# First layer's gate/up of a two-layer FFN kernel: seven of its eleven tiles as seven block products each

## The chip, the cores and the metric

One core of a Trainium2 chip runs the whole program. The metric is the device time of one execution in microseconds (us); three executions of the kernel before give 455.81, 456.37 and 456.49, median 456.37.

## The reference, cut to what matters

Two layers are applied to x of 8 x 128 tokens (1,024) by 512 features, each as x + ffn(cond(x)). The part that changes is the first gated FFN, whose weights come as 4-bit numbers ("nibbles"), packed by eight in a 32-bit word, with a zero point and a scale for each group of 128 input rows.

```python
def _dequant(qw, qz, sc, g_idx):
    wq = qw[:, None, :] >> shifts[None, :, None] & NIB
    zq = qz[:, :, None] >> shifts[None, None, :] & NIB   # + 1.0
    return sc[g_idx] * (wq - zq[g_idx])
w_gu = _dequant(qweight_gu, qzeros_gu, scales_gu, g_idx_gu)   # 512 x 2752
inter = einsum('bsh,hf->bsf', y, w_gu)                        # y = _L0_cond_ref(x, ...)
gate, up = inter[..., :1376], inter[..., 1376:]
h = silu(gate) * up
w_d = _dequant(qweight_down, qzeros_down, scales_down, g_idx_down)
x = x + einsum('bsf,fh->bsh', h, w_d)
x = x + _L1_ffn_ref(_L1_cond_ref(x, ...), ...)                # plain weights, 512 -> 1792 -> 512
```

## The kernel before

Everything is held transposed: features on the 128 partitions, 1,024 tokens along the row, in two halves of 512 (one PSUM bank each). fp32 accuracy comes from splitting every operand into a rounded part (hi, made by ScalarE, helper `hi`, L658) and a remainder (lo, made by VectorE, helper `lo`, L967) and taking three products: w_hi v_hi, w_hi v_lo, w_lo v_hi (`mm3`, L1443, L1444, L1447). A 128x128 block of weights against 1,024 tokens is thus six matmuls of 512 columns.

The order on each engine is the order in which the code issues it; engines are tied by semaphores alone. The stages on TensorE: ten warming matmuls; routing, LoRA and base product of the first condition layer, which leaves y in the banks 0/1, 4/5, 6/7 and 2/3 (`lora`, in this order; each increments `s_y`); the first gate/up, eleven tiles of 128 hidden features (FT0 = 11); the first down projection in six chunks (`d0_tile`, chunks of 4, 4 and 3 tiles for each of two pairs of outputs); the second condition layer (`z_product`); the second gate/up in 14 tiles, which is already done by seven block products each (`product`, `p_1` to `p_7`); the second down projection, in block products too.

A first gate/up tile (`gate_up`) is eight weight blocks (gate and up, four of each), 48 matmuls. It uses banks 0 to 3 for even tiles and 4 to 7 for odd ones. Around it:

- SyncE loads the packed weights of one tile at a time (`load_qw`, L416), and in the last third of the stage the packed down weights (`load_qd`, L434, through three slots, the fourth load waiting for `s_dn`, the count of dequantized down rows), then x again for the residual (L440).
- GpSimd gathers, by indirect DMA (helper `gather`, L579), four times 256 scales a tile (`scales_gu`) and two rows of down tables after it (`tables_dn`).
- VectorE takes the nibbles out of the bytes (L1080), adds the zeros (L1084) and multiplies by the scales (`dequant_gu`, L1087, increments `s_wf`); makes lo of the weights (`w_lo`), multiplies silu(gate) by up (`gu_step`, L1115), makes lo of the result, and dequantizes the eleven rows of down weights (`dequant_dn`, L1095 to L1109) between the last tiles. `w_lo_dn(e)` makes lo of the weights of down chunk e.
- ScalarE makes hi of y, weights and result, and silu (L715).

The tiles 2 to 9 run in a hardware loop on SyncE, TensorE, ScalarE and VectorE.

The second gate/up shows what a block tile is. Weights are a 2 x 2 arrangement of 256 x 128 blocks A11, A12, A21, A22, activations one of B11, B12, B21, B22. GpSimd makes four sums of weight blocks (`sums`, L616 to L621: S1 = A21+A22, S3 = A11-A21, S2 = S1-A11, S4 = A12-S2), four sums of activation blocks are made once, and seven products of six matmuls each give what eight gave. Products share banks, so ScalarE copies partial results out between them (`snap_1`, `snap_5`, `snap_2`) and VectorE adds them (`c_11`, `c_12`, `c_22`), and the last product of a tile, `p_4`, is issued behind `p_1` of the next tile. Its hi and lo of weights are 1,792 columns wide, where a plain tile has 1,024.

## Time and profile before

| | us |
|---|---|
| median of three executions (455.81 to 456.49) | 456.37 |
| the profiled execution's own time | 457.44 |
| its span, first to last instruction | 455.6 |
| TensorE busy in the span | 449.1 |
| VectorE, ScalarE, GpSimd busy | 319.3, 195.2, 172.8 |
| first gate/up stage on TensorE, 45.01 to 165.62 | 120.6 |

The page's times are of one execution. Busy time counts overlapping matmuls once. 'Idle before' is the time that the engine stood still ahead of a group, and the arrow says what ended it. Columns of an instruction row: start, duration, engine, line, operation, output <- input, shape, count, and idle time before it in brackets. A matmul of 512 columns is shown as 0.39 us, but the next starts 0.23 us after it, since they are pipelined.

### The profile page before, as it was taken

How to read it: one execution, taken by the hardware profiler on the slowest of the kernel's cores; microseconds unless marked ns; L12 is line 12 of the kernel's file. 1: busy time of each engine (PE TensorE's matmuls, PEld its weight loads, DVE VectorE, ACT ScalarE, POOL GpSimd, SP SyncE). 2: the span in 40 equal slices, each digit the busy share in tenths (PEclk: the TensorE clock that was granted, in tenths of full speed). 3: DMA queues.
4: the chain of work that ended last, by engine and by line, in shares of the span. 5: the costliest groups of instructions: out<-in, count | busy, mean ns of one | idle time of the engine just before them, and what ended most of it. 6: DMA issues, size and time to landing. Idle time of an engine off the chain costs nothing.

```text
span 455.6 us, 5596 instructions
## 1 busy us (share of the span) xinstructions
PE 449.1 (99%) x1988; PEld 366.5 (80%) x1988; DVE 319.3 (70%) x420; ACT 195.2 (43%) x247; POOL 172.8 (38%) x160
## 2 busy tenths in 40 slices
PE   8999999999999999999999999999999999999996
PEld 4688887888888888888888778888888888888885
DVE  3864845555557998746687768868788578999921
ACT  4513423233222224235666756556465545474200
POOL 3254774743330000900002779795987500000000
PEclk9999999999999999999999999999999999999999
DMA  8262443441315236276358824947749146885623
GB/s 263 81 192 77 133 142 95 137 124 58 127 46 208 71 91 280 82 288 229 106 195 304 331 81 143 303 129 270 260 140 306 62 161 255 312 307 174 221 102 130
DMA packets 32357, 79.93 MB, mean 175 GB/s; under 512 B 3232, under 2 KB 17728, under 8 KB 30800
## 3 DMA queue, kind: packets, MB, share of 16 engines
q1 hardware_dynamic: 28128, 68.05, 43.2%
q0 software_dynamic: 3632, 10.84, 7.5%
q10 hardware_dynamic: 576, 0.79, 0.5%
q8 instruction: 10, 0.16, 0.1%
q14 instruction: 11, 0.09, 0.1%
HBM read 58.95 MB, written 20.72 MB: 175 GB/s over the span
## 4 chain that ended last, share of the span: by engine, by line
PE 96%; DMA 2%; ACT 1%; SPq 0%; issue 0%; DVE 0%
PE ps L1443 15%; PE ps L1447 15%; PE ps L1444 15%; PE ps L1612 10%; PE ps L1613 10%; PE ps L1614 10%; PE ps L1715 5%; PE ps L1714 5%; PE ps L1716 5%; DMA res<-in_xT 2%; PE ps L1595 2%; PE ps L1593 2%; PE ps L1594 2%; PE ps L1601 1%; ACT act_hi L658 0%; SPq L398 0%
## 5 line engine op out<-in xcount | busy, mean ns | idle before, releaser
L1443 PE MATMUL ps<-h_hi,ring_hi 128*128 128x512 f32 x264 | 102.7, 389 | 0.0
L1444 PE MATMUL ps<-h_lo,ring_hi 128*128 128x512 f32 x264 | 102.7, 389 | 0.0
L1447 PE MATMUL ps<-h_hi,ring_lo 128*128 128x512 f32 x264 | 82.3, 389 | 0.8 <-issue 0.8
L579 POOL DMA_INDIRECT raw<-in_sc_gu,idx_gu x44 | 47.9, 1088 | 42.1 <-DVE ring_lo L967 20.6
L1443 PEld LDWEIGHTS ps<-h_hi,ring_hi 128*128 128x128 f32 x264 | 49.6, 188 | 10.8 <-issue 0.5
L1447 PEld LDWEIGHTS ps<-h_hi,ring_lo 128*128 128x128 f32 x264 | 49.6, 188 | 10.7 <-issue 0.5
L1444 PEld LDWEIGHTS ps<-h_lo,ring_hi 128*128 128x128 f32 x264 | 49.6, 188 | 10.3
L1612 PE MATMUL ps<-zt_hi,ring_hi 128*128 128x512 f32 x140 | 54.6, 390 | 0.1
L658 ACT ACTIVATE ring_hi<-raw 128x1792 fp32r<-128x1792 f32 (+1 forms) x23 | 32.1, 1398 | 52.3 <-PE ps L1447 30.9
L1614 PE MATMUL ps<-zt_hi,ring_lo 128*128 128x512 f32 x140 | 54.5, 389 | 0.0
L1613 PE MATMUL ps<-zt_lo,ring_hi 128*128 128x512 f32 x140 | 54.5, 389 | 0.0
L967 DVE TENSOR_TENSOR ring_lo<-raw,ring_hi 128x1792 fp32r<-128x1792 f32 (+1 forms) x23 | 42.2, 1835 | 7.1 <-ACT ring_hi L658 7.1
L1115 DVE TENSOR_TENSOR sil<-sil,ps 128x1024 f32<-128x1024 f32 x11 | 13.4, 1221 | 35.9 <-PE ps L1447 25.7
L1612 PEld LDWEIGHTS ps<-zt_hi,ring_hi 128*128 128x128 f32 x140 | 26.3, 188 | 6.0 <-issue 0.5
L1614 PEld LDWEIGHTS ps<-zt_hi,ring_lo 128*128 128x128 f32 x140 | 26.3, 188 | 5.5
L1613 PEld LDWEIGHTS ps<-zt_lo,ring_hi 128*128 128x128 f32 x140 | 26.3, 188 | 5.4
L1714 PE MATMUL ps<-slot,wd 128*128 128x512 f32 x70 | 27.2, 389 | 0.0
L1716 PE MATMUL ps<-slot,wd 128*128 128x512 f32 x70 | 27.2, 389 | 0.0
L715 ACT ACTIVATE sil<-ps 128x1024 f32<-128x1024 f32 x11 | 11.3, 1027 | 31.3 <-PE ps L1447 21.0
L967 DVE TENSOR_TENSOR ad_lo<-ad_raw,ad_hi 128x1024 fp32r<-128x1024 f32 x15 | 19.4, 1328 | 5.5 <-ACT ad_hi L658 5.5
L1612 PE MATMUL ps<-ze_hi,ring_hi 128*128 128x512 f32 x56 | 22.1, 394 | 0.0
L1614 PE MATMUL ps<-ze_hi,ring_lo 128*128 128x512 f32 x56 | 21.8, 390 | 0.0
(218 smaller groups left out, 873.8 us busy)
## 6 DMA issues: line engine op xcount, KB each, us to landing
ad_raw<-in_w1T SPq DMA_DIRECT2D x8, 1024.0 KB, 4.9
wd<-down_weights SPq DMA_DIRECT2D x7, 1024.0 KB, 5.7
...
```

The lines of the kernel that those rows point to most:

```text
L579: pool.indirect_dma_start(dst, None, table, bass.IndirectOffsetOnAxis(ap=index, axis=0)).then_inc(done, 16)
L658: act.activation(dst, src, ACT.Copy).then_inc(done, 1)
L967: dve.tensor_tensor(dst, src, hi_part.bitcast(F32), ALU.subtract).then_inc(done_sem, 1)
L1443: pe.matmul(ps[:, bank + hf, :], w_hi, v_hi[:, t], start=first, stop=False)
L1444: pe.matmul(ps[:, bank + hf, :], w_hi, v_lo[:, t], start=False, stop=False)
L1447: ins = pe.matmul(ps[:, bank + hf, :], w_lo, v_hi[:, t], start=False, stop=last)
L1612: pe.matmul(ps[:, bank, :], ring1_hi[s][:, w], z_hi[:, t], start=first and k == 0, stop=False, skip_group_check=True)
L1613: pe.matmul(ps[:, bank, :], ring1_hi[s][:, w], z_lo[:, t], start=False, stop=False, skip_group_check=True)
L1614: ins = pe.matmul(ps[:, bank, :], ring1_lo[s][:, w], z_hi[:, t], start=False, stop=k == 1, skip_group_check=True)
L1714: pe.matmul(ps[:, bank, :], w_hi, v_hi, start=k == 0 and i in (1, 2, 3, 5), stop=False, skip_group_check=True)
L1715: pe.matmul(ps[:, bank, :], w_hi, v_lo, start=False, stop=False, skip_group_check=True)
L1716: return pe.matmul(ps[:, bank, :], w_lo, v_hi, start=False, stop=k == DH - 1, skip_group_check=True)
```

## The change

Tiles 2 to 8 of the first gate/up (BLOCK_TILES) are computed by seven block products of six matmuls; tiles 0, 1, 9 and 10 stay plain, with gate and up as functions of their own. For it:

- y is copied out of PSUM (`y_copy`), its four block sums are made by VectorE and split (`y_sum_hi`, `y_sum_lo`). TensorE waits with the first gate for the first of these copies, since its banks are read by it.
- GpSimd makes the weight sums of each block tile (`sums` with `blocks0`) between the gathers of scales. Weight and partial-result buffers are laid out anew.
- All packed weights of the stage are loaded by two DMAs at the start, their nibbles taken out in two VectorE instructions and the zeros added in three, where each tile had one of either.
- Gathers of down tables and loads of packed down weights wait for the last seventh product (`s_p[7]` >= 7). The reload of x is issued behind the load of row 4.
- The loops of this stage are gone on all engines; semaphores shared with the second layer's tiles count on from NS = 7.
- ScalarE makes hi of down chunk 2 before adapter 0, not behind it.

The diff, cut to its core:

```diff
+PLAIN = (0, 1, FT0 - 2, FT0 - 1)
+SC_KB = tuple((64, 112)[i % 2] if i != FT0 - 2 else 196 for i in range(FT0))
+
+
 HI_FRAME = (2, 3, 5, 6, 8, 9, 11)
...
+            return h_hi[:, YT + m, t], h_lo[:, YT + m, t]
+
+        def w_col(block, k):
+
+            if block in S_COL:
+                return S_COL[block] + P * k
+            return {B_A11: 0, B_S4: P, B_A12: 4 * P, B_A22: 5 * P}[block] + 2 * P * k
+
+        def blocks0(s):
+
+            w = raw0[s][:, 0:8 * P].rearrange("p (k g n) -> p k g n", k=KD, g=2)
+            s1, s2, s3 = (raw0[s][:, S_COL[b]:S_COL[b] + 2 * P].rearrange("p (k n) -> p k n", k=2) for b in (B_S1, B_S2, B_S3))
+            return w[:, 0:2, 1, :], w[:, 0:2, 0, :], w[:, 2:4, 0, :], w[:, 2:4, 1, :], s1, s2, s3, w[:, 0:2, 1, :]
+
         def g_bank(s, x):
...
-                load_qw(i, i)
-            with loop(sp, 0, (FT0 - 3) // 2) as j:
-                for s in range(2):
-                    need(sp, s_nib, 2 * j + s + 1)
...
             for k in range(3):
                 load_qd(k)
-            need(sp, s_wf, FT0)
-            sp.dma_start(res[:, :, :], a["xT"]).then_inc(s_xr, 16)
-
-
             sp.wait_ge(s_aok, 1)
             rows = [sp.value_load(aid[0:1, 2 * NBATCH + b:2 * NBATCH + b + 1], min_val=0, max_val=NBATCH - 1)
...
@@ -450,6 +487,11 @@
             for k in range(3, FT0):
                 sp.wait_ge(s_dn, k - 2)
                 load_qd(k)
+                if k == 4:
+                    sp.wait_ge(s_wf, FT0)
+                    sp.wait_ge(s_hm0, NS)
+                    sp.wait_ge(s_hm1, NS)
+                    sp.dma_start(res[:, :, :], a["xT"]).then_inc(s_xr, 16)
             sp.wait_ge(s_ring, FT0)
             for b in range(2):
                 load_adapter(b)
...
+            def sums(n, a21, a11, a12, a22, s1, s2, s3, s4):
+
                 pool.tensor_tensor(s1, a21, a22, ALU.add).then_inc(s_sum[1], 1)
                 pool.tensor_tensor(s3, a11, a21, ALU.subtract).then_inc(s_sum[3], 1)
                 pool.wait_ge(s_sum[1], n)
                 pool.tensor_tensor(s2, s1, a11, ALU.subtract).then_inc(s_sum[2], 1)
+                pool.wait_ge(s_sum[3], n)
                 pool.wait_ge(s_sum[2], n)
                 pool.tensor_tensor(s4, a12, s2, ALU.subtract).then_inc(s_sum[4], 1)
+
+            def blocks1(w):
+
+                return (w[:, i, :] for i in range(8))
+
+            for i in range(4):
+                scales_gu(i)
+            for i in BLOCK_TILES:
+                pool.wait_ge(s_wf, i + 1)
+                sums(sum_at("q", i), *blocks0(i % 2))
+                if i + 2 < FT0:
+                    scales_gu(i + 2)
+            pool.wait_ge(s_p[7], NS)
+            tables_dn(0, 5)
+            pool.wait_ge(s_ring, BLOCK_TILES[-1] + 1)
+            tables_dn(5, FT0)
 
...
-                need(act, s_ring, q - 1)
-                hi(ring_hi[:, s, 0:width], raw[:, s, 0:width], s_whi)
-
-            def w_hi_gu(i, s):
-                w_hi(i, s, 1024, s_wf, i + 1)
+            def y_copy(m, b, value):
+                act.wait_ge(s_ylo, value)
+                act.activation(halves(y_raw[:, m, :]), ps[:, b:b + 2, :], ACT.Copy).then_inc(s_yr, 1)
+
+            def y_sum_hi(i):
+                act.wait_ge(s_yt, i)
+                hi(y_sum(yt_hi, i), y_low(yt_raw, i), s_yth)
+
+            def w_hi(i):
+
+                if i in BLOCK_TILES:
+                    act.wait_ge(s_sum[3], sum_at("q", i))
+                    act.wait_ge(s_sum[4], sum_at("q", i))
+                    n = 14 * P
+                else:
...
-                for s in range(2):
-                    i = 2 * j + s
-                    gu_step(i, s, 0, lambda: w_hi_gu(i + 2, s))
-            gu_step(FT0 - 3, 0, 0, lambda: w_hi_gu(FT0 - 1, 0))
-            gu_step(FT0 - 2, 1, 0, lambda: w_hi_dn(0))
-            gu_step(FT0 - 1, 0, 0, lambda: None)
+            y_copy(3, 2, KD)
+            y_copy(1, 4, KD)
+            y_copy(2, 6, KD)
+            y_sum_hi(1)
+            silu(0)
+            y_sum_hi(2)
+            w_hi(2)
+            y_sum_hi(3)
+            y_sum_hi(4)
+            h_split(0)
+            silu(1)
+            for i in BLOCK_TILES:
+                y_snap_1(i)
+                w_hi(i + 1)
+                y_snap_5(i)
+                h_split(i - 1)
+                y_snap_2(i)
+                y_silu_0(i)
+                y_silu_1(i)
+            w_hi(FT0 - 1)
+            h_split(FT0 - 3)
+            silu(FT0 - 2)
+            w_hi_dn(0)
+            h_split(FT0 - 2)
+            silu(FT0 - 1)
+            h_split(FT0 - 1)
             w_hi_dn(1)
 
 
...
 
             def pre_split(g):
 
-                act.wait_ge(s_sum[3], g + 1)
-                act.wait_ge(s_sum[4], g + 1)
+                act.wait_ge(s_sum[3], sum_at("w", g))
+                act.wait_ge(s_sum[4], sum_at("w", g))
...
+            NIB_PARTS = ((0, 5), (5, FT0))
+
+            def nibbles(part):
+
+                i0, i1 = NIB_PARTS[part]
+                m = m16[:, i0:i1, :, :].rearrange("p i g w -> p (i g w)")
+                dve.tensor_scalar(m, m, sh16, 0x0F0F, ALU.logical_shift_right, ALU.bitwise_and).then_inc(s_nib, 1)
+
+            dve.wait_ge(s_sh, 16)
+            dve.wait_ge(s_qw, 32)
+            nibbles(0)
             dve.wait_ge(s_gTp, 1)
             dve.wait_ge(s_hAc, 1)
             dve.tensor_tensor(halves(hg_full), ps[:, 2:4, :], halves(hA_full), ALU.mult).then_inc(s_hg, 1)
+            nibbles(1)
             dve.wait_ge(s_hghi, 1)
             lo(hg_lo, hg_full, hg_hi, s_hglo)
...
-                n2 = nib_gu[s].bitcast(U16).rearrange("p (g w) -> p g w", g=2 * KD)
-                dve.tensor_tensor(n2, n2, zg16[:, :, bass.ds(i * 64, 64)], ALU.add).then_inc(s_n, 1)
-                need(dve, s_n, i + 1)
-                need(dve, s_raw["gu0"][s], (i - s) * 32 + 64)
-                dve.scalar_tensor_tensor(out=raw[:, s, :], in0=nib_gu[s], scalar=16.0, in1=raw[:, s, :], op0=ALU.subtract,
-                                         op1=ALU.mult).then_inc(s_wf, 1)
+            zg16 = zg.bitcast(U16).rearrange("p (g i w) -> p i g w", g=2 * KD, i=FT0)
+            ZERO_PARTS = ((0, 2), (2, 5), (5, FT0))
+
+            def add_zeros(part):
+
+                i0, i1 = ZERO_PARTS[part]
+                dve.wait_ge(s_nib, 2 if i1 == FT0 else 1)
+                dve.tensor_tensor(m16[:, i0:i1], m16[:, i0:i1], zg16[:, i0:i1], ALU.add).then_inc(s_n, 1)
+
+            def dequant_gu(i):
+
+                s = i % 2
+                dve.wait_ge(s_n, sum(i >= i0 for i0, _ in ZERO_PARTS))
+                need(dve, s_wlo, i - 1)
...
+                dve.wait_ge(s_s5, frame(i) + 1)
+                dve.tensor_tensor(snap0[i % 2][:, 2, :], ps[:, y_bank(i % 2, 0), :], snap0[i % 2][:, 2, :], ALU.add).then_inc(s_c22, 1)
+
+            def y_mul_0(i):
+                dve.wait_ge(s_silu0, frame(i) + 1)
+                dve.wait_ge(s_ring, i + 1)
+                dve.tensor_tensor(h_raw[:, i, first], snap0[i % 2][:, 0, :], ps[:, y_bank(i % 2, 0), :], ALU.mult).then_inc(s_hm0, 1)
+
...
                 dve.wait_ge(s_whi, Q["d0"] + e + 1)
                 lo(d0_ring(ring_lo, e), d0_unit(e), d0_ring(ring_hi, e), s_wlo)
 
 
-            dequant_gu(0, 0)
...
+            w_lo(0)
+            dequant_gu(1)
+            add_zeros(2)
+            w_lo(1)
             y_split(0, 0)
-            w_lo(0, 0, 1024)
             y_split(1, 4)
+            dequant_gu(2)
             y_split(2, 6)
             y_split(3, 2)
-            dequant_gu(1, 1)
-            w_lo(1, 1, 1024)
-            dequant_gu(2, 0)
-            for i in range(2):
-                gu_step(i, i, 0, Q["gu0"], lambda: w_lo(i + 2, i, 1024))
-                dequant_gu(i + 3, 1 - i)
-            with loop(dve, 1, FT0 // 2 - 1) as j:
-                for s in range(2):
-                    i = 2 * j + s
-                    gu_step(i, s, 0, Q["gu0"], lambda: w_lo(i + 2, s, 1024))
-                    dequant_gu(i + 3, 1 - s)
-            dequant_dn(0)
-            gu_step(FT0 - 3, 0, 0, Q["gu0"], lambda: w_lo(FT0 - 1, 0, 1024))
-            for k in range(1, 4):
+            b11, b12 = y_raw[:, 0:2, first], y_raw[:, 0:2, second]
+            b21, b22 = y_raw[:, 2:4, first], y_raw[:, 2:4, second]
+            dve.wait_ge(s_yr, 3)
+            dve.tensor_tensor(y_low(yt_raw, 1), b12, b11, ALU.subtract).then_inc(s_yt, 1)
+            dve.wait_ge(s_yr, KD)
+            dve.wait_ge(s_yt, 1)
+            dve.tensor_tensor(y_low(yt_raw, 2), b22, y_low(yt_raw, 1), ALU.subtract).then_inc(s_yt, 1)
+            dve.tensor_tensor(y_low(yt_raw, 3), b22, b12, ALU.subtract).then_inc(s_yt, 1)
+            dve.wait_ge(s_yt, 2)
+            dve.tensor_tensor(y_low(yt_raw, 4), b21, y_low(yt_raw, 2), ALU.subtract).then_inc(s_yt, 1)
+            y_sum_lo(1)
+            y_sum_lo(2)
+            gate_times_up(0)
+            w_lo(2)
+            dequant_gu(3)
+            y_sum_lo(3)
+            y_sum_lo(4)
+            h_split(0)
+            for i in BLOCK_TILES:
+                dequant_gu(i + 2)
+                if i > 2:
+                    y_mul_0(i - 1)
+                else:
+                    gate_times_up(i - 1)
+                w_lo(i + 1)
+                y_c_11(i)
+                h_split(i - 1)
+                y_c_12(i)
+                y_c_22(i)
+                y_mul_1(i)
+            y_mul_0(FT0 - 3)
+            w_lo(FT0 - 1)
+            h_split(FT0 - 3)
+            for k in range(4):
                 dequant_dn(k)
-            gu_step(FT0 - 2, 1, 0, Q["gu0"], lambda: w_lo_dn(0))
-            for k in range(4, 7):
+            gate_times_up(FT0 - 2)
+            w_lo_dn(0)
+            h_split(FT0 - 2)
+            for k in range(4, 8):
                 dequant_dn(k)
-            gu_step(FT0 - 1, 0, 0, Q["gu0"], lambda: dequant_dn(7))
+            gate_times_up(FT0 - 1)
+            h_split(FT0 - 1)
             w_lo_dn(1)
 
...
+                    c = slice(2 * P * k, 2 * P * k + P)
+                    ins = mm3(4 * s, ring0_hi[s][:, c], ring0_lo[s][:, c], y_hi[:, k, :], y_lo[:, k, :], k == 0, k == KD - 1)
+                if KD - 1 in ks:
+                    ins.then_inc(s_gate, 1)
+
+            def up(i):
+
+                s = i % 2
+                for k in range(KD):
...
+
+                bank = y_bank(s, x)
+                for k in range(2):
+                    c = w_col(W_OF[i], k)
+                    w_hi, w_lo = ring0_hi[s][:, c:c + P], ring0_lo[s][:, c:c + P]
+                    v_hi, v_lo = y_block(right, k) if isinstance(right, str) else (y_sum(yt_hi, right)[:, k], y_low(yt_lo, right)[:, k])
+                    pe.matmul(ps[:, bank, :], w_hi, v_hi, start=first_in_bank and k == 0, stop=False, skip_group_check=True)
+                    pe.matmul(ps[:, bank, :], w_hi, v_lo, start=False, stop=False, skip_group_check=True)
+                    ins = pe.matmul(ps[:, bank, :], w_lo, v_hi, start=False, stop=k == 1, skip_group_check=True)
+                return ins
+
+            def sum_ready(i):
+                pe.wait_ge(s_yth, i)
+                pe.wait_ge(s_ytl, i)
+
+            def y_p_1(i):
+                weights_ready(i)
+                if i < 4:
+                    pe.wait_ge(s_hm, i - 1)
+                need(pe, s_hm0, frame(i) - 1)
+                y_product(1, i % 2, 0, True, "b11").then_inc(s_p[1], 1)
+
+            def y_p_4(i):
+                sum_ready(4)
+                pe.wait_ge(s_c22, frame(i) + 1)
...
+                pe.wait_ge(s_s5, frame(i) + 1)
+                y_product(3, i % 2, 2, False, "b22").then_inc(s_p[3], 1)
+
+            def y_p_7(i):
+                sum_ready(3)
+                pe.wait_ge(s_s2, frame(i) + 1)
+                y_product(7, i % 2, 0, False, 3).then_inc(s_p[7], 1)
+
+            def banks_free(n):
+                pe.wait_ge(s_hm0, n)
+                pe.wait_ge(s_c11, n)
+                pe.wait_ge(s_c12, n)
+
+            weights_ready(0)
+            pe.wait_ge(s_yr, 1)
+            gate(0, range(KD), s_ylo)
+            pe.wait_ge(s_yr, 2)
+            up(0)
+            weights_ready(1)
+            pe.wait_ge(s_yr, KD)
+            gate(1, range(KD))
+            up(1)
+            for i in BLOCK_TILES:
+                y_p_1(i)
+                if i > BLOCK_TILES[0]:
...
+                y_p_3(i)
+                y_p_7(i)
+            weights_ready(FT0 - 2)
+            banks_free(NS - 1)
+            gate(FT0 - 2, range(1))
+            y_p_4(FT0 - 3)
+            gate(FT0 - 2, range(1, KD))
+            up(FT0 - 2)
+            weights_ready(FT0 - 1)
+            banks_free(NS)
+            gate(FT0 - 1, range(KD))
+            up(FT0 - 1)
 
             def d0_tile(e, k, m, hfs):
```

## Rows read from the trace of the kernel before

**Rows 1.** The page: busy time by engine, and the chain that ended last.
```profile
PE 449.1 (99%) x1988; PEld 366.5 (80%) x1988; DVE 319.3 (70%) x420; ACT 195.2 (43%) x247; POOL 172.8 (38%) x160
...
PE 96%; DMA 2%; ACT 1%; SPq 0%; issue 0%; DVE 0%
```

**Rows 2.** Timeline of TensorE at the first tile: starts of two groups of six.
```profile
45.01 0.39 PE L1443 MATMUL ps<-h_hi,ring_hi 128*128 128x512 f32 x1
...
46.37 0.39 PE L1443 MATMUL ps<-h_hi,ring_hi 128*128 128x512 f32 x1
```

**Rows 3.** Timeline of TensorE in tile 2, the first one in the loop.
```profile
70.40 0.39 PE L1447 MATMUL ps<-h_hi,ring_lo 128*128 128x512 f32 x1
71.54 0.39 PE L1447 MATMUL ps<-h_hi,ring_lo 128*128 128x512 f32 x1 [0.76 <-issue]
```

**Rows 4.** Timeline of ScalarE in the second gate/up: snap_1 of two tiles, between them hi, snap_5, snap_2.
```profile
299.59 0.60 ACT L832 ACTIVATE snap<-ps 128x512 f32<-128x512 f32 x1 [1.36 <-PE ps L1614]
301.04 1.71 ACT L658 ACTIVATE ring_hi<-raw 128x1792 fp32r<-128x1792 f32 x1 [0.84 <-PE ps L1614]
302.65 0.57 ACT L842 ACTIVATE snap<-ps 128x512 f32<-128x512 f32 x1
305.03 0.60 ACT L837 ACTIVATE snap<-ps 128x512 f32<-128x512 f32 x1 [1.81 <-PE ps L1614]
...
309.11 0.60 ACT L832 ACTIVATE snap<-ps 128x512 f32<-128x512 f32 x1 [0.85 <-PE ps L1614]
```

**Rows 5.** Groups of GpSimd by line and shape: busy, mean ns | idle before.
```profile
L579 POOL DMA_INDIRECT raw<-in_sc_gu,idx_gu x44 | 47.9, 1088 | 42.1 <-DVE ring_lo L967 20.6 <-issue 13.1 <-PE ps L1447 5.3
L617 POOL TENSOR_TENSOR raw<-raw 128x256 f32<-128x256 f32 x12 | 19.6, 1632 | 0.0
L621 POOL TENSOR_TENSOR raw<-raw 128x256 f32<-128x256 f32 x12 | 18.9, 1573 | 0.9
L619 POOL TENSOR_TENSOR raw<-raw 128x256 f32<-128x256 f32 x12 | 11.1, 929 | 0.0
L616 POOL TENSOR_TENSOR raw<-raw 128x256 f32<-128x256 f32 x12 | 10.2, 848 | 13.4 <-DMA raw<-in_gu 13.1
```

**Rows 6.** Timeline of GpSimd: a sum alone, a sum beside VectorE, two gathers.
```profile
260.53 0.74 POOL L617 TENSOR_TENSOR raw<-raw 128x256 f32<-128x256 f32 x1
...
181.13 1.64 POOL L616 TENSOR_TENSOR pre_raw<-pre_raw 128x256 f32<-128x256 f32 x1 [50.30 <-DVE ring_lo L967]
...
30.39 0.95 POOL L579 DMA_INDIRECT raw<-in_sc_gu,idx_gu  x1 [0.30 <-issue]
31.65 1.63 POOL L579 DMA_INDIRECT raw<-in_sc_gu,idx_gu  x1 [0.30 <-issue]
33.58 0.95 POOL L579 DMA_INDIRECT raw<-in_sc_gu,idx_gu  x1 [0.30 <-issue]
```

**Rows 7.** Timeline of VectorE beside them, and the first multiplication by scales.
```profile
180.97 6.25 DVE L967 TENSOR_TENSOR ad_lo<-ad_raw,ad_hi 128x1024 fp32r<-128x1024 f32 x4
...
31.23 1.23 DVE L967 TENSOR_TENSOR h_lo<-sil,h_hi 128x1024 fp32r<-128x1024 f32 x1 [1.13 <-ACT h_hi L658]
...
36.88 1.23 DVE L1087 SCALAR_TENSOR_TENSOR raw<-res,raw 128x1024 f32<-128x1024 uint8 x1 [3.30 <-DMA raw<-in_sc_gu,idx_gu]
```

**Rows 8.** Groups of VectorE by line and shape: busy, mean ns | idle before.
```profile
L967 DVE TENSOR_TENSOR ring_lo<-raw,ring_hi 128x1792 fp32r<-128x1792 f32 x12 | 28.8, 2396 | 5.8 <-ACT ring_hi L658 5.8
L967 DVE TENSOR_TENSOR h_lo<-sil,h_hi 128x1024 f32 x6 | 7.4, 1226 | 1.3 <-ACT h_hi L658 1.1 <-issue 0.2
L1084 DVE TENSOR_TENSOR res<-res 128x512 uint16<-128x512 uint16 x11 | 4.7, 426 | 1.0
L1258 DVE TENSOR_TENSOR snap<-ps,snap 128x512 f32<-128x512 f32 x14 | 9.7, 691 | 8.5 <-PE ps L1614 8.4
```

**Rows 9.** Timeline of ScalarE: hi of the first quarter of y.
```profile
41.13 1.03 ACT L658 ACTIVATE h_hi<-ps 128x1024 fp32r<-128x1024 f32 x1 [9.94 <-PE ps L1447]
```

**Rows 10.** Timeline of VectorE: first instructions of two down rows, then w_lo_dn(1).
```profile
150.25 0.48 DVE L1095 TENSOR_SCALAR dn_work<-dn_work,shifts 128x512 uint32<-128x512 uint32 x1
...
152.68 0.48 DVE L1095 TENSOR_SCALAR dn_work<-dn_work,shifts 128x512 uint32<-128x512 uint32 x1
...
170.66 1.23 DVE L967 TENSOR_TENSOR ring_lo<-dn_work,ring_hi 128x1024 fp32r<-128x1024 f32 x1
```

More of the change, by code:

```diff
@@ L40 @@
 FT1 = F1 // P
-CH0 = (6, 5)
 NPAIR = NBATCH // 2
@@ L332, in z_bank, with y_bank, frame, plain @@
             return Z_BANK[b]
+        def y_bank(s, x):
+            return 4 * s + x
+        def frame(i):
+            return BLOCK_TILES.index(i)
+        def plain(i):
+            return PLAIN.index(i)
+        def y_sum(t, i):
+            return t[:, i - 1]
+        def y_low(t, i):
+            return t[:, i % 4]
+        def y_block(b, k):
+            m, t = {"b11": (k, first), "b21": (2 + k, first), "b22": (2 + k, second)}[b]
+            return h_hi[:, YT + m, t], h_lo[:, YT + m, t]
[7 more added lines that the diff above has]
+            return w[:, 0:2, 1, :], w[:, 0:2, 0, :], w[:, 2:4, 0, :], w[:, 2:4, 1, :], s1, s2, s3, w[:, 0:2, 1, :]
         def g_bank(s, x):
@@ L355, in d0_unit, with table_group @@
             return tab_dn[:, k0:k0 + D0_CHUNK[c], BLK * pr:BLK * pr + BLK]
+        def table_group(k):
+            return sum(k >= sum(D0_CHUNK[:c]) for c in range(1, len(D0_CHUNK)))
         def d0_ring(ring, e):
@@ new lines, in h_split, with y_snap_1 @@
+            def h_split(i):
+                if i in BLOCK_TILES:
+                    act.wait_ge(s_hm0, frame(i) + 1)
+                    act.wait_ge(s_hm1, frame(i) + 1)
+                    hi(h_hi[:, i, :], h_raw[:, i, :], s_hhi)
+                else:
+                    act.wait_ge(s_hm, plain(i) + 1)
+                    hi(h_hi[:, i, :], sil[i][:, :], s_hhi)
+            def y_snap_1(i):
+                act.wait_ge(s_p[1], frame(i) + 1)
+                need(act, s_hm0, frame(i) - 1)
+                act.activation(snap0[i % 2][:, 0, :], ps[:, y_bank(i % 2, 0), :], ACT.Copy).then_inc(s_s1, 1)
@@ L958, in _, with mark @@
             done = [0]
+            def mark(ins):
+                done[0] += 1
+                return ins.then_inc(s_v, 1)
             def own(ins):
```

323 lines of the change are left out of this document (172 added, 151 removed).

## The prediction, made before the change was run

> **What bounds the kernel now.** I read the page's busy times first, then its chain: TensorE is busy in 449.1 of 455.6 us and holds 96% of the chain that ended last [rows 1]. So time goes only if TensorE gets less work, or if it stands still. Next its timeline: six matmuls, one weight block against 1,024 tokens, start 1.36 us apart (45.01 to 46.37) [rows 2]. In the whole stage it stands still once, in tile 2: a matmul starts at 71.54 where 70.40 + 0.23 = 70.63 was due, released by "issue", not by data, with hardly more than 0.9 us lost [rows 3]. No other engine holds it there. Last, the second gate/up, which already runs in block products: its snap_1 come at 299.59 and 309.11, 9.52 us apart, which is 7 x 1.36 [rows 4]. That stage is the pattern for what the new tiles do on TensorE, ScalarE and VectorE.
>
> **Part 1, fewer products: -9.5 us.** A plain tile is 8 x 1.36 = 10.88 us, a block tile 9.52 [rows 2, 4]. Seven tiles save 7 x 1.36 = 9.52 us, 42 of 1,988 matmuls. That a block product is no slower than its six matmuls is what the 9.52 us of the second layer show.
>
> **Part 2, no loop in this stage: -0.9 us.** The pause of 71.54 - 70.63 = 0.9 us lies in the loop's first pass, and the straight code around it has none [rows 3]. It could stay (straight code is longer to fetch), so 0 to -0.9; I take it whole.
>
> **Part 3, start of the stage: +0.8 us (0 to 2).** TensorE comes free for tile 0 at 45.01 [rows 2]. It now also waits for y_copy(0) on ScalarE, which waits for lo of the first y quarter on VectorE, and VectorE has both dequantizations, both w_lo and the zero additions queued ahead of that. The last release among these is a gather. GpSimd no longer waits for the router and can start scales right behind its last small DMA, near 26.3. A gather is issued each 1.25 us (30.39 to 31.65), some take 0.6 more [rows 6]; with one such in each four, tile 0's are out at 31.9 and tile 1's at 37.1. Landing: the last gather of tile 0 ended at 33.58 + 0.95 = 34.53 and VectorE went on at 36.88, 2.35 later [rows 6, 7]. So tile 1's scales are there at 39.4. Behind them: multiplication 1.2, zeros of six tiles, w_lo(1) 1.2, lo of y 1.2, y_copy 1.03 and two handovers of 0.1. The zeros: 512 columns of 16 bits took 0.43 [rows 8], some 0.15 of it fixed (estimate), so 3,072 take 1.8. Sum 39.4 + 6.6 = 46.0 less the overlaps of 0.1 to 0.2 between VectorE instructions: 45.8. Hi of y starts at 41.13 now [rows 9] and isn't the last. The nibble instructions lie before and behind the LoRA product, hidden by the wait for scales even if they take twice what I give them (1 us each). The two loads of 0.7 MB stand behind x in SyncE's queue; their cover is that nothing needs them before 27, and without it they would push this chain by their landing. The other copies of y are read in time: the first `up` needs banks 2/3 only 5.4 us later. The work behind (block sums of y, four 1,024-wide instructions each for sum, hi and lo, some 14 us in all) has the 21.8 us of tiles 0 and 1 as cover.
>
> **Part 4, block tiles beside GpSimd: +1.9 us (0 to 5).** VectorE per tile, with the rows' means: multiplication by scales 1.23, w_lo 2.4, lo of h 1.23, three adds and two products of about 0.7 each: 8.3 of 9.52 us [rows 7, 8]. ScalarE: 1.71 + 3 x 0.6 + 1.06 + 2 x 0.62 = 5.8 [rows 4]. Both fit. GpSimd is the tight one: four sums and four gathers. The means of the second layer's sums are 0.85 + 1.63 + 0.93 + 1.57 = 5.0 us; a gather is 1.09 + 0.30 of issue, four 5.5 [rows 5]. That is 10.5 us, more than the tile's 9.52. The means hold collisions: a sum is 0.74 alone and 1.64 beside VectorE instructions that read two SBUF tensors, one of 1.23 of which then becomes 6.25 / 4 = 1.56; a gather is 0.95 or 1.63 [rows 6, 7]. The lower bound is 4 x 0.74 + 4 x 1.25 = 8.0. In this loop VectorE's two-SBUF instructions are about 5 of 9.5 us, but shorter ones (1.2) than the 2.5 us ones that the second layer's sums run into. Placing them one by one: w_lo and lo of h fall on the gathers (+0.5 us each, less 0.1), the multiplication on one or two sums (+0.9 to +1.5). That gives 9.8 to 10.1; I take P = 9.9.
>
> What P costs: sums(3) can start only when VectorE has dequantized tile 3, behind the y work, at 62.7, and in collision takes 4 x 1.65, so ends at 69.3 (clock of before, part 3's shift left out). Sums(8), five rounds later, ends at 69.3 + 5P. Behind it until p_4(7) may start: hi 1.8, w_lo 2.0, c_11, lo of h, c_12, c_22: 7.0 us. Undisturbed, p_4(7) starts at 45.01 + 21.76 + 8.16 + 5 x 9.52 + 1.36 = 123.9. Delay = 69.3 + 5P + 7.0 - 123.9 = 5P - 47.6: 1.9 at 9.9; nothing at 9.5; 4.9 at 10.5. It comes as some 0.4 us per tile, with VectorE's c_22 ahead of p_4.
>
> The Trainium skill, GPSIMD Engine Reference, section Key points, says that GpSimd shares its SBUF interfaces with VectorE and contends with instructions that have two SBUF inputs; it speaks against moving sums into this stage. The trace agrees (0.74 against 1.64), and shows the gathers' instructions longer too. By that rule alone the sum would be nearer to P = 10.5, -3.3 us in all; by the placement above it is -6.3.
>
> **Part 5, down tables behind the tiles: +1.4 us (0 to 3).** Let Z be the end of p_7(8). New waits: GpSimd and SyncE for s_p[7] >= 7, behind which stand all down gathers, and on SyncE x's reload and the adapters. Four rows of gathers take 5.2 us and land 2.35 later: Z + 7.7. VectorE is free at Z + 6.5. A row costs 152.68 - 150.25 = 2.43 us [rows 10], four 9.7: Z + 17.4. Then gate_times_up(9), w_lo_dn(0) and lo of tile 9 (3 x 1.2), four more rows to Z + 30.7, then the product of tile 10, ready at Z + 23.3 but last in VectorE's queue, its hi and lo, and w_lo_dn(1): Z + 35.4. TensorE from Z: gate and up of tiles 9 and 10 and p_4, 17 x 1.36 = 23.1; down chunk 0, 8 x 1.36 = 10.9: it wants chunk 1 at Z + 34.0. It waits 1.4 us. Before, w_lo_dn(1) was done at 171.9 [rows 10] and wanted at 165.6 + 10.9 = 176.5, 4.6 us ahead; all of that cover is used. Next, chunk 2: rows 8 to 10 (7.3), hi and lo end at Z + 44.6, wanted at 46.3. Chunk 3, behind two adapters on both engines: 52.4 against 54.5. Both just hidden, as ScalarE makes chunk 2 before the adapter. Everything further hangs on TensorE's own counts and shifts with it. Rows 5 and on come behind x's 2 MB on SyncE (7.6 us) but are wanted at Z + 23 at the earliest.
>
> **Sum.** -9.5 - 0.9 + 0.8 + 1.9 + 1.4 = -6.3 us. Against the profiled execution's own time, 457.44 (span 455.6 and 1.84 around it), 451.1; the median of the runs is 1.07 lower, 456.37, which gives **450.1 us**.
>
> **The rivals.**
> 1. *All cover holds*: GpSimd needs no more than 9.5 us a tile, VectorE gets to the down rows in time. For it: 8.0 us without collisions [rows 6]. Against it: the means of 10.5 [rows 5]. Time 456.4 - 10.4 + 0 to 1.5: 446.0 to 447.5, centre 447.
> 2. *GpSimd at its means*, P = 10.5: 3.0 us more than my forecast, 453.1. For it: rows 5 as they stand, measured beside a like VectorE load.
> 3. *GpSimd paces the whole stage, slower than before*: the place is sums and gathers against VectorE, the price 5P - 47.6, and it decides from P = (47.6 + 8.2 + 0.9) / 5 = 11.3. If sums keep 5.0 and every gather takes 1.5 + 0.3 [rows 5, 6], P = 12.2, a delay of 13.4 instead of 1.9: 461.6. Against it: a mean gather is 1.09 with VectorE half busy.
> 4. *The saving isn't there*: block products leave a gap at each change of bank, so a tile takes 10.88 still. The second layer's 9.52 [rows 4] speaks against it; it would give 450.1 + 9.5 = 459.6.
>
> **How the numbers follow.** Forecast 0.50 (448 to 452), rival 1 0.24, rival 2 0.19, rival 3 0.04, rival 4 0.01, and 0.02 for nearly nothing gained. Differences under 0.2% (0.9 us) can't be told from no change here. Faster 0.93, same 0.02, slower 0.05. Range 446.6 to 454.0: it takes in rival 1's centre and rival 2, with parts 3 and 5 at their upper ends in part.
>
> **What would show it.** Tile 0 of gate/up starting on TensorE near 45.8; snap_1 of block tiles 9.5 apart up to tile 4 and about 9.9 from there; TensorE's waits named VectorE adds in the block tiles, about 2 us in all; one wait of 1 to 2 us for ring_lo at down chunk 1, and none at chunks 2 and 3; 1,946 matmuls; no pause by "issue" near 71. Wrong would make it: GpSimd sums beyond 5 us a tile, a wait for scales on VectorE that holds products behind it, instruction fetch in the straight code, or loads of packed weights that slow x at the start.

## The result, and the profile after

The changed kernel takes **461.09 us** (median of 4 runs, 460.69 to 463.71) against 456.38 (455.81 to 456.49) before: ratio 1.0118, 95% interval 1.008 to 1.0156. It is 1.2% slower where 1.4% faster was forecast. The profiled execution took 461.01 us, its span is 459.2. Ratios and intervals leave out the two executions that took over 1.5% more than the fastest of their kernel, one of before (463.34 us) and one of experiment 8 (457.44 us).

The page after: busy time, granted clock by slices, the chain that ended last, the costliest GpSimd group (busy, mean ns | idle before).
```profile
PE 444.0 (97%) x1946; PEld 358.4 (78%) x1946; DVE 343.7 (75%) x439; ACT 218.9 (48%) x283; POOL 216.9 (47%) x187
...
PEclk9999999999999998999999999999999999999999
...
PE 71%; POOL 15%; issue 7%; DVE 4%; DMA 1%; ACT 1%; POOLq 0%; ACTq 0%; DVEq 0%
...
L620 POOL DMA_INDIRECT scale<-in_sc_gu,idx_gu x44 | 59.9, 1361 | 12.3 <-issue 11.7
```
TensorE has 42 matmuls less, and its busy time is 5.1 us less than in [rows 1], not 9.5. It held 96% of the chain; now 15% is GpSimd's and 7% "issue". The same 44 gathers take 59.9 us of GpSimd instead of 47.9 [rows 5]. And one slice of the clock is under full speed; before, none was.

What TensorE waited for, by releaser (us in total, times, longest):
```profile
PE ps L1611 <- issue: 3.5, 1, 3.5
PE ps L1611 <- DVE h_lo L1067: 3.1, 1, 3.1
PE ps L1725 <- ACT snap L795: 3.1, 4, 1.3
```
Its timeline places them: tile 0, the four waits of the third product (p_3, which adds to the bank that snap_5 reads first; the first wait is shown, in tile 4), and down chunk 1.
```profile
47.66 0.47 PE L1611 MATMUL ps<-h_hi,ring_hi 128*128 128x512 f32 x1 [3.15 <-DVE h_lo L1067]
...
95.48 0.50 PE L1725 MATMUL ps<-h_hi,ring_hi 128*128 128x512 f32 x1 [1.33 <-ACT snap L795]
...
178.67 0.51 PE L1611 MATMUL ps<-h_hi,ring_hi 128*128 128x512 f32 x1 [3.48 <-issue]
```
And the windows of TensorE around them (window: its length, busy us and matmuls, granted clock, DMA share, GB/s):
```profile
47.66:164.15 116.49, 113.13 (x486) 1.00 0.28 91
164.15:178.67 14.52, 11.05 (x49) 1.00 0.61 216
178.67:182.10 3.43, 3.43 (x9) 0.54 1.01 420
```
From this the account. **Start:** 47.66 against 45.01 [rows 2], +2.65. **Stage:** gate and up of 11 tiles are 4 x 10.88 + 7 x 9.52 = 110.16 us of matmuls and took 116.49 (chunk 0 starts at 164.15), +6.33. The four waits show only half of that, 3.1 us: each is counted from the end shown for the matmul before, 0.16 us behind the time at which the next was due, and pauses of 0.1 to 0.2 us follow in the same product and the next, some 0.5 us a tile. The first matmuls of p_3 start at 95.48, 106.23, 117.20 and 128.15, 10.75, 10.97 and 10.95 us apart. **Down chunk 1:** wanted at 164.15 + 10.88 = 175.03, started at 178.67, +3.64. **Clock:** behind that stand TensorE ran 3.43 us at 0.54 of full speed, the lower of its two levels (1.2 GHz) for nearly all of it: 3.43 x 0.46 = +1.6. The sum is +14.2, less the 9.5 and 0.9 won: +3.8; the span grew by 3.6.

### The profile page after: what moved, and what is told of

Read it like the earlier page. It is cut to its first block, busy times and chain, and to the rows that moved or that the text cites. A ratio compares the mean times of both kernels' runs of the same rounds, so it can differ in the third digit from the quotient of the medians.

```text
span 459.2 us, 5528 instructions
## 1 busy us (share of the span) xinstructions
PE 444.0 (97%) x1946; PEld 358.4 (78%) x1946; DVE 343.7 (75%) x439; ACT 218.9 (48%) x283; POOL 216.9 (47%) x187
## 4 chain that ended last, share of the span: by engine, by line
PE 71%; POOL 15%; issue 7%; DVE 4%; DMA 1%; ACT 1%; POOLq 0%; ACTq 0%; DVEq 0%
PE ps L1865 10%; PE ps L1867 10%; PE ps L1866 10%; POOL scale L620 8%; PE ps L1611 6%; PE ps L1612 6%; PE ps L1615 6%; PE ps L1968 5%; PE ps L1967 5%; PE ps L1969 5%; PE ps L1848 2%; PE ps L1846 2%; PE ps L1847 2%; POOL raw L648 2%; POOL raw L651 2%
## 5 line engine op out<-in xcount | busy, mean ns | idle before, releaser
L1611 PE MATMUL ps<-h_hi,ring_hi 128*128 128x512 f32 x152 | 60.0, 395 | 6.6 <-issue 3.5
L620 POOL DMA_INDIRECT scale<-in_sc_gu,idx_gu x44 | 59.9, 1361 | 12.3 <-issue 11.7
L1612 PE MATMUL ps<-h_lo,ring_hi 128*128 128x512 f32 x152 | 59.9, 394 | 0.0
L1067 DVE TENSOR_TENSOR ring_lo<-raw,ring_hi 128x1792 fp32r<-128x1792 f32 (+1 forms) x23 | 45.5, 1978 | 17.6 <-ACT ring_hi L704 17.4
L704 ACT ACTIVATE ring_hi<-raw 128x1792 fp32r<-128x1792 f32 (+1 forms) x23 | 36.6, 1592 | 41.1 <-POOL raw L651 15.8
L1615 PE MATMUL ps<-h_hi,ring_lo 128*128 128x512 f32 x152 | 48.2, 392 | 0.0
L1611 PEld LDWEIGHTS ps<-h_hi,ring_hi 128*128 128x128 f32 x152 | 28.9, 190 | 13.4 <-issue 7.4
L1612 PEld LDWEIGHTS ps<-h_lo,ring_hi 128*128 128x128 f32 x152 | 29.0, 191 | 6.0
L1615 PEld LDWEIGHTS ps<-h_hi,ring_lo 128*128 128x128 f32 x152 | 28.8, 190 | 6.1
L1865 PEld LDWEIGHTS ps<-zt_hi,ring_hi 128*128 128x128 f32 x140 | 26.3, 188 | 6.3 <-issue 0.8
L1866 PEld LDWEIGHTS ps<-zt_lo,ring_hi 128*128 128x128 f32 x140 | 26.3, 188 | 5.5
L1867 PEld LDWEIGHTS ps<-zt_hi,ring_lo 128*128 128x128 f32 x140 | 26.3, 188 | 5.4
L651 POOL TENSOR_TENSOR raw<-raw 128x256 f32<-128x256 f32 x19 | 25.7, 1352 | 2.7
L648 POOL TENSOR_TENSOR raw<-raw 128x256 f32<-128x256 f32 x19 | 24.7, 1298 | 0.0
L645 POOL TENSOR_TENSOR raw<-raw 128x256 f32<-128x256 f32 x19 | 18.1, 954 | 12.1 <-DMA raw<-in_gu 11.1
```

The costliest lines, as they stand in the source:

```text
L620: pool.indirect_dma_start(dst, None, table, bass.IndirectOffsetOnAxis(ap=index, axis=0)).then_inc(done, 16)
L651: pool.tensor_tensor(s4, a12, s2, ALU.subtract).then_inc(s_sum[4], 1)
L704: act.activation(dst, src, ACT.Copy).then_inc(done, 1)
L1067: dve.tensor_tensor(dst, src, hi_part.bitcast(F32), ALU.subtract).then_inc(done_sem, 1)
L1611: pe.matmul(ps[:, bank + hf, :], w_hi, v_hi[:, t], start=first, stop=False)
L1612: pe.matmul(ps[:, bank + hf, :], w_hi, v_lo[:, t], start=False, stop=False)
```

## The experiments

The times are medians. The kernel before, run beside them, took 456.34 us (experiments 1 to 4), 456.65 (5 to 8) and 456.87 (9). In experiments with added lines a statement's line number is 1 to 17 higher than in the changed kernel. `...` marks what is cut.

**1. Fewer gathers on GpSimd.** The table and VectorE's wait count change with it.
```diff
...
+                if i >= 4:
+                    gather(scale[i][:, :], a["sc_rep"], idx_gu[:, i, 0:1], s_raw["gu0"][i % 2])
+                    return
                 for k in range(KD):
...
```


> The changed kernel, 461.1 us, but the scales of tiles 4 to 10 come by one gather of 1,024 columns instead of four of 256 (three of the four index look-ups are left out, which for these inputs name the same group). Theory A, GpSimd paces the block tiles (its round is 10.95 us for sums and gathers, TensorE's 9.52): the round falls to about 4.6 + 1.6 = 6 us, snap_5 and the third product no longer wait, the 6.3 us that the stage is longer than its matmuls go, about 455 us. Rival B, the order on ScalarE or the load of VectorE holds the tiles: under 1 us of gain, above 460.

Measured 455.42 us (453.79 to 457.08), ratio 0.9977 [0.9955, 1.0]: 5.7 us less than the changed kernel. The rounds of GpSimd, first of the changed kernel (one whole round: the first sum, the four gathers, the next first sum), then of this one:
```profile
99.57 0.74 POOL L645 TENSOR_TENSOR raw<-raw 128x256 f32<-128x256 f32 x1
...
104.06 0.95 POOL L620 DMA_INDIRECT scale<-in_sc_gu,idx_gu  x1
105.32 0.95 POOL L620 DMA_INDIRECT scale<-in_sc_gu,idx_gu  x1 [0.30 <-issue]
106.58 2.00 POOL L620 DMA_INDIRECT scale<-in_sc_gu,idx_gu  x1 [0.30 <-issue]
108.88 1.43 POOL L620 DMA_INDIRECT scale<-in_sc_gu,idx_gu  x1 [0.30 <-issue]
110.33 0.75 POOL L645 TENSOR_TENSOR raw<-raw 128x256 f32<-128x256 f32 x1
```
VectorE beside the last two gathers, w_lo and lo of h:
```profile
105.73 2.03 DVE L1067 TENSOR_TENSOR ring_lo<-raw,ring_hi 128x1792 fp32r<-128x1792 f32 x1 [1.82 <-ACT ring_hi L704]
...
108.27 1.22 DVE L1067 TENSOR_TENSOR h_lo<-h_raw,h_hi 128x1024 fp32r<-128x1024 f32 x1
```
With one gather:
```profile
92.72 0.74 POOL L648 TENSOR_TENSOR raw<-raw 128x256 f32<-128x256 f32 x1 [2.85 <-DVE raw L1203]
...
97.49 1.81 POOL L620 DMA_INDIRECT scale<-in_sc_rep,idx_gu  x1
102.24 0.74 POOL L648 TENSOR_TENSOR raw<-raw 128x256 f32<-128x256 f32 x1 [2.94 <-DVE raw L1203]
```
In the changed kernel GpSimd has no idle time but issue: it sets the round, 10.76 us here, 10.74 to 10.95 in the others from tile 4 on (the round before them, from tile 3's sums to tile 4's beside VectorE's work on y, took 13.26). With one gather it waits 2.9 us for VectorE in each of these rounds, the round is 102.24 - 92.72 = 9.52 us, TensorE's own, and the four waits of the third product are gone. GpSimd's pace is the largest loss, and fewer gathers remove it: they are 6.3 us of the round.

The same trace shows the clock's price: here it was at half from the end of the stand at tile 0 on, and chunk 1's stand of 3.0 us left it at 1.00.
```profile
47.55:53.40 5.85, 5.85 (x14) 0.50 0.22 70
53.40:160.50 107.10, 107.10 (x474) 1.00 0.28 95
```
5.85 us at half clock are 2.9 us lost. Its ten runs differ by mean clock: 453.8 to 454.2 us at 0.996, 455.2 to 457.1 at 0.992 or 0.993. Before ran at 0.998 to 1.000 in all but two of its runs.

**2. Order at the start.** The low halves of y ahead of the second tile's low weights and of the zeros; on ScalarE the high halves of y ahead of the second tile's high weights.
```diff
...
             dequant_gu(1)
-            add_zeros(2)
-            w_lo(1)
             y_split(0, 0)
...
+            dequant_gu(2)
+            w_lo(1)
+            add_zeros(2)
...
```


> The changed kernel with VectorE's lo of y directly behind the multiplication of tile 1, and w_lo(1), the zeros of tiles 5 to 10 and tile 2 behind them (ScalarE alike). Theory A, tile 0 starts 3.3 us late because of what is queued ahead of lo of y: start at 45 instead of 47.7, and the whole kernel follows, about 458.4 us. Rival B, GpSimd paces the block tiles whatever the start: the gain is given back as longer waits in tiles 4 to 8, 460.5 to 461.

Measured 460.15 us (459.18 to 462.01), ratio 1.0095 [1.0065, 1.0125]. What TensorE waited for:
```profile
PE ps L1725 <- ACT snap L795: 4.5, 6, 1.7
PE ps L1611 <- issue: 3.5, 1, 3.5
...
PE ps L1611 <- DVE h_lo L1067: 0.2, 1, 0.2
```
Tile 0 starts at 44.75, 2.9 us sooner, but the third products now wait 4.5 us in six tiles in place of 3.1 in four, and chunk 1 starts at 178.85, no sooner than in the changed kernel (178.67): GpSimd, whose sums start no sooner (121.45 against 121.28 for tile 8), takes the whole gain back, as rival B had it. The 1.6 us by which the profiled execution is shorter are the clock's, which fell behind no stand here (mean 0.999).

**3. The packed weights' loads behind the store of the zeros.**
```diff
+            sp.wait_ge(s_zk, 16)
             for hp in range(2):
```


> The changed kernel with the two loads of packed weights issued only when the zeros are stored. Theory: these 1.4 MB make the store land 2.2 us later (4.15 us of wait against 1.97) and with it every gather behind it; the first gather of scales starts 1.5 to 2 us earlier, tile 0 1.5 us earlier, about 459.6 us. Rival: the nibbles then come late for VectorE and hold the LoRA product, no gain or slower than 461.

Measured 459.27 us (458.17 to 459.79), ratio 1.0067 [1.0051, 1.0084]. Tile 0 starts at 45.54. The first gather of the zeros, which waits for their store, in the changed kernel, then here:
```profile
22.16 1.02 POOL L620 DMA_INDIRECT res<-zeros_gu,idx_gu  x1 [4.15 <-DMA zeros_gu<-zu]
```
```profile
19.79 1.02 POOL L621 DMA_INDIRECT res<-zeros_gu,idx_gu  x1 [1.97 <-DMA zeros_gu<-zu]
```
The store of 11 KB, issued at 17.44, stood behind 1.4 MB of packed weights, issued at 6.1, and landed 2.2 us later, and with it came every gather of the start. Taking these loads away wins 2.1 us of tile 0's start, the order of experiment 2 won 2.9; the late start (2.65) needed both causes, and either mend removes most of it. But this one also brings GpSimd forward: tile 8's sums start at 119.60 in place of 121.28 and chunk 1 at 176.00 in place of 178.67, so here the gain came through.

**4. Order at the end of the stage.** In the changed kernel TensorE's wait at chunk 1 ends 0.1 us behind this row, the low half of its weights, which is last in VectorE's queue:
```profile
177.35 1.22 DVE L1067 TENSOR_TENSOR ring_lo<-dn_work,ring_hi 128x1024 fp32r<-128x1024 f32 x1
```
It is moved ahead on VectorE (shown), and the high half likewise on ScalarE:
```diff
...
             for k in range(4, 8):
                 dequant_dn(k)
+            w_lo_dn(1)
             gate_times_up(FT0 - 1)
             h_split(FT0 - 1)
-            w_lo_dn(1)
...
```


> The changed kernel with lo and hi of down chunk 1 put ahead of the product and split of tile 10 on VectorE and ScalarE. Theory A, TensorE's wait of 3.6 us at chunk 1 is VectorE's queue order: the wait and the 3.4 us of half clock behind it (1.7 us) go, about 1.3 us come back at chunk 2, which wants what the same queue makes: about 457 us. Rival B, it is the late tables and loads (rows wait for DMA twice) and the same time comes back as a wait at chunk 2: 460 to 461.

Measured 458.89 us (457.54 to 460.17), ratio 1.0057 [1.004, 1.0074]. TensorE waits 0.63 us at chunk 1 and 0.97 at chunk 2: 2.0 of 3.6 us won. That is theory A's mechanism, but not its 457 us: the half clock was not saved, it lay behind tile 0's stand of 3.0 us in this trace; the one run with a mean clock of 1.000 took 457.54.

**5. The same, and x's reload four table rows later** (`k == 8` in place of `k == 4` on SyncE).

> Two edits at the end of the stage: the weights of the second down chunk ahead of the last tile's product of gate and up, and the 2 MB reload of x started after table row 8's wait instead of row 4's. With the first edit alone 458.89 us were measured, with waits of 0.63 us (second chunk) and 0.97 us (third chunk) left. Theory (the reload delays table row 5 by 1.4 us and with it what follows on VectorE): the wait for row 5 goes, the wait at the second chunk goes too, 457.9 to 458.5 us. Rival 1 (the row is late by its own gathers): unchanged, 458.7 to 459.1 us. Rival 2 (x is needed as early as before): its wait appears where x is added and the run is above 459.5 us.

Measured 457.46 us (455.24 to 458.25), ratio 1.001 [0.9995, 1.0025], 1.4 us less than with the order alone. Chunk 1 waits no more; chunk 2 waits 0.72 and chunk 4 0.52, where it waited for nothing before. The row that was late in the changed kernel, on VectorE:
```profile
167.09 0.49 DVE L1208 TENSOR_SCALAR dn_work<-dn_work,shifts 128x512 uint32<-128x512 uint32 x1 [1.43 <-DMA dn_work<-in_qw_dn]
```
It stood behind x's 2 MB, issued at 155.15. Here that wait is gone. The reload's price is 1.4 us by the medians, and 1.05 by the traces, in which chunk 2 starts at 187.77 in place of 188.82.

**6. Is it ScalarE's order?** snap_5 ahead of the high half of the next weights.
```diff
...
                 y_snap_1(i)
-                w_hi(i + 1)
                 y_snap_5(i)
+                w_hi(i + 1)
...
```


> One edit: in the block tiles, ScalarE reads the second product's sums (snap_5) ahead of the high half of the next tile's weights instead of behind it. Theory (GpSimd paces the block tiles, one round of 10.95 us made of four sums and four gathers, and nothing in it waits for ScalarE): the starts of the sums stay 10.7 to 11.0 us apart, the waits of the third product go away but come back ahead of the next tile's first product, and only part of the 3.1 us is won: 459.5 to 461.1 us. Rival (the order of ScalarE is the cause): all 3.1 us of the third products' waits are won and the rounds fall under 10.3 us: 458 us or less.

Measured 464.75 us (463.41 to 466.0), ratio 1.0187 [1.0156, 1.0218]. The rival falls by the rounds: the part of my theory that they stay holds (sums start at 81.23, 92.16, 102.88, 113.85, 124.80); its number does not, 3.7 us more came. In the trace tile 4's sums start 3.35 us later than in the changed kernel, and 2.16 of that were lost ahead of the edited lines: ScalarE made the high half of y's third quarter late, and the low halves, tile 3's weights and tile 3's sums (66.78 in place of 64.62) followed. The changed kernel, then this one:
```profile
47.30 1.94 ACT L704 ACTIVATE h_hi<-ps 128x1024 fp32r<-128x1024 f32 x2
```
```profile
49.98 1.94 ACT L704 ACTIVATE h_hi<-ps 128x1024 fp32r<-128x1024 f32 x2 [3.02 <-remote]
```
So the run can't say what the edit itself costs. GpSimd's first sum of tile 3, and VectorE beside it:
```profile
66.78 5.06 POOL L645 TENSOR_TENSOR raw<-raw 128x256 f32<-128x256 f32 x1 [9.33 <-DVE raw L1200]
71.79 0.74 POOL L646 TENSOR_TENSOR raw<-raw 128x256 f32<-128x256 f32 x1
```
```profile
66.61 2.36 DVE L1067 TENSOR_TENSOR yt_lo<-yt_raw,yt_hi 128x1024 fp32r<-128x1024 f32 x2
68.88 1.22 DVE L1067 TENSOR_TENSOR h_lo<-sil,h_hi 128x1024 fp32r<-128x1024 f32 x1
70.02 1.22 DVE L1200 SCALAR_TENSOR_TENSOR raw<-nib,scale 128x1024 f32<-128x1024 uint8 x1
```
A sum of 0.74 us that started 0.17 us behind a VectorE instruction took 5.06 us, until VectorE's chain of four was over at 71.2. In the changed kernel the same sum started 0.16 us behind the same instruction and took 1.65, while VectorE's pair took 2.89 in place of 2.36:
```profile
64.62 1.65 POOL L645 TENSOR_TENSOR raw<-raw 128x256 f32<-128x256 f32 x1 [0.39 <-DVE raw L1200]
```
```profile
64.46 2.89 DVE L1067 TENSOR_TENSOR yt_lo<-yt_raw,yt_hi 128x1024 fp32r<-128x1024 f32 x2
```
What picks between the two isn't shown. The net loss is small, 0.6 us, since the three sums behind the long one then took 0.74 each. The medians differ by more than the traces (3.7 against 2.4 us): two of the four runs have a mean clock of 0.988 and 0.989 and took 466 us.

**7. All three mended**, with one gather for a tile's scales.

> All three late points mended together: tiles 4 to 10 get their scales by one gather of 1,024 columns in place of four; the low half of y ahead of the second tile's weights, and nibbles loaded behind the store of the zeros; down weights ahead of the last product and the reload of x later. Theory (the three points are separate, and each given gain was taken back only by GpSimd's pace): from 455.4 us with the one gather, minus 2.7 (start at 44.8 in place of 47.5 us) and minus 3.0 (second down chunk): 449 to 450.5 us, with no wait of the third products and rounds of 9.5 us. Rival (something else takes the place, VectorE at the start, or the clock falls for other reasons): 452 us or more.

Measured 452.83 us (450.25 to 456.68), ratio 0.9926 [0.9899, 0.9953]. The median lies in the rival's range, and the runs say why: 450.25 and 452.96 us at clock 1.000, 451.75 to 454.41 at 0.995 to 0.999, 455.26 to 456.68 at 0.992. The profiled one (0.992) has two stands, each with half clock behind it: 1.88 us at tile 0 and 2.15 at tile 2's p_3, behind a first sum of tile 3 that took 5.06 us as in experiment 6. The stand at tile 0 is ScalarE's: it started the first high half of y at 42.91 where the next experiment's trace has 40.77, with TensorE's matmuls in the same places. What held ScalarE I can't name; experiment 6's trace has the like.

**8. All three mended, nothing repeated:** tiles 2 to 7 get their scales in pairs, by four gathers of 512 columns for each pair; those of tile 8 are fetched ahead of tile 2's sums.

> As the kernel with all three points mended, but nothing of the table is repeated: the scales of tiles 2+3, 4+5 and 6+7 come by four gathers of 512 columns for each pair (a table that holds each tile's scales beside the next one's), those of 8, 9 and 10 by four of 256 as before: 24 gathers from tile 2 on in place of 36. Theory (what counts on GpSimd is the number of gather instructions, the time of one grows little from 256 to 512 columns; 1,024 columns took 1.68 us against 1.09 us for 256): between the sums of tile 2 and of tile 8 GpSimd has 6 x 4.7 of sums and 12 to 16 gathers of 1.2 to 1.5 us, less than the 57 us of the matmuls, so 449 to 451.5 us. Rival (the time goes by the bytes gathered): the pace of 10.9 us returns in some rounds and the run is at 453 us or more.

Measured **451.54 us** (six runs, 450.37 to 457.44), ratio 0.9899 [0.9861, 0.9936]: 1% faster than before, 2% faster than the changed kernel. The theory's 449 to 451.5 holds within 0.04 us. GpSimd's gathers by form, and TensorE's waits:
```profile
L623 POOL DMA_INDIRECT scale<-in_sc_gu,idx_gu x20 | 23.8, 1189 | 5.8 <-issue 5.6
L623 POOL DMA_INDIRECT scale<-in_sc_two,idx_gu x12 | 16.1, 1341 | 5.7 <-issue 3.2 <-DVE yt_raw L1303 2.5
```
```profile
PE ps L1740 <- ACT snap L805: 1.8, 1, 1.8
...
PE ps L1626 <- issue: 0.6, 1, 0.6
```
Twice the columns cost 1.34 us in place of 1.19, and in experiment 1 a gather of 1,024 columns, with no VectorE instruction beside it that reads two SBUF tensors, took what one of 256 takes alone, 0.95:
```profile
73.35 0.95 POOL L620 DMA_INDIRECT scale<-in_sc_rep,idx_gu  x1 [0.16 <-issue]
```
GpSimd pays by the instruction, hardly by the byte. The 32 gathers took 39.9 us in place of 59.9 for 44. Left are 0.6 us at chunk 2 and 1.79 us at tile 2's p_3, which waits by way of ScalarE for tile 3's sums.

**9. The fourth gather of pair 4+5 split off**, to take those 1.79 us:
```diff
...
-                if i in (2, 4, 5, 8):
-                    scales_gu({2: 4, 4: 6, 5: 9, 8: 10}[i])
+                if i in (2, 3):
+                    scales_gu(4, (range(0, 3), range(3, KD))[i - 2])
+                if i in (4, 5, 8):
...
```


> As the kernel with tile pairs, but the four gathers of the pair 4+5 are split: three ahead of tile 3's sums and one behind them. In the pair kernel tile 3's sums started at 66.52 us, 1.96 us after tile 3's weights were there (64.56), behind the fourth gather; TensorE then stood 1.79 us for tile 3's second sum and its clock was at half for 3.4 us. Theory: the sums start near 64.7, the pause goes and with it the clock drop: 1.8 + 1.7 = 3.5 us less than 451.5, so 448 to 450 us. Rival (tile 4's weights, now later by the fourth gather's landing, are late in their turn): a pause of 1 us or more appears at tile 4, 451 us or more.

Measured 456.97 us (453.75 to 460.47), ratio 0.9998 [0.9966, 1.0029]. The rival holds:
```profile
78.36 1.23 DVE L1217 SCALAR_TENSOR_TENSOR raw<-nib,scale 128x1024 f32<-128x1024 uint8 x1 [4.86 <-DMA scale<-in_sc_two,idx_gu]
...
82.44 0.77 PE L1742 MATMUL ps<-yt_hi,ring_hi 128*128 128x512 f32 x1 [3.47 <-ACT snap L802]
```
Tile 4's weights wait for the fourth gather and TensorE stands 3.47 us. This profile also has the late ScalarE at the start (42.77), with a stand of 3.31 us at tile 0, so the 456.97 us are not all the edit's.

## Why the prediction was wrong, by its own steps

**Part 1** (-9.5) was right: 1,946 matmuls, and the 9.52 us of experiment 1's rounds. **Part 2** (-0.9) was right: no "issue" pause in the gate/up tiles.

**Part 3** (+0.8, measured +2.65) failed in its cover: "nothing needs them before 27" asked who reads the packed weights, not what stands behind them. The zeros' store did; it landed in 4.15 us where before it took 1.97, and the first scales' gather went out at 28.07 where I had 26.3. Tile 1's multiplication came at 41.18, 1.8 later than my 39.4, and that is the whole miss: with the loads behind the store tile 0 starts at 45.54, forecast 45.8. I had named loads slowing x as the danger; it was the store.

**Part 4** (+1.9, measured +6.3) is the term that decided: mechanism right, size wrong. I took P = 9.9 between 8.0 and the means' 10.5. It was 10.85 (sums starting at 77.88 and 121.28 are four rounds apart), above the upper of them. The 9.9 was low by its own terms already: 8.0 with +0.9 for the gathers and +0.9 to +1.5 for the sums is 9.8 to 10.4, not 9.8 to 10.1. The step that failed is "w_lo and lo of h fall on the gathers (+0.5 us each, less 0.1)": the gather beside w_lo took 2.00 us in place of 0.95, the next, beside lo of h, 1.43, together +1.5 instead of +0.9. The sums of tiles 5 to 8 took 4.3 to 4.6 in place of 3.0, +1.3 to +1.6, the upper end of what I gave them. With both measured the placement gives 10.8 to 11.1. By my own formula 5 x 10.85 - 47.6 = 6.7; measured 6.3. The waits appeared where forecast, in the block tiles, but by another link: not VectorE's adds ahead of p_4, but ScalarE's snap_5 ahead of p_3. It stands behind the high half of the next tile's weights, which waits for GpSimd.

The Trainium skill, GPSIMD Engine Reference, section Key points, says that GpSimd shares its SBUF interfaces with VectorE and contends with instructions that have two SBUF inputs. The traces agree: a sum of 0.74 us took 1.65 in the changed kernel and 5.06 in experiment 6. It was the better guide: "by that rule alone", with the means of [rows 5], I had put the sum "nearer to P = 10.5, -3.3 us in all", and set it aside for a placement.

**Part 5** (+1.4, measured +3.64): the chain is the one forecast, but two links were late (row 5 is the sixth, counted from 0). With Z at 164.15 - 23.1 = 141.0, the first row came at Z + 9.4 (150.42) instead of Z + 7.7, and "rows 5 and on come behind x's 2 MB ... but are wanted at Z + 23 at the earliest" was wrong in its conclusion: row 5 came at Z + 26.1, 1.43 us late. The rows themselves were 0.9 us cheaper in eight, and 1.7 + 1.43 - 0.9 is the miss of 2.2. Chunks 2 and 3 did not wait, as forecast, but behind a stand of 3.6 us at chunk 1 that is no test of the forecast: with chunk 1 mended, chunk 2 waited 0.97 and 0.72 us (experiments 4 and 5).

**What the sum lacked:** the clock, +1.6. The profiled run of before [rows 1] had no long stand and no slice under full speed, so nothing in its trace priced one. In the changed kernel the stand of 3.5 us at chunk 1 cost 5.1.

Rival 3, GpSimd as the pace with a run slower than before, is the one that came. That its 461.6 us is so near to 461.09 is luck: it stood on P = 12.2, with parts 3 and 5 as forecast and no clock. It was to decide from P = 11.3, and P was only 10.85, because I held parts 3 and 5 at their middle values. Parts 3, 4 and 5 weren't independent: all three rest on when gathers and small transfers get through beside other work, and all three came out above even the upper ends (2, 5 and 3). Adding these ends gives -0.4, and the clock makes that a loss. A chance of 0.04 had them fail one at a time.
